# A four-layer attention kernel: the first pair's mask and matrix added by GpSimd to ScalarE's copy

## The chip, the cores and the metric

The kernel runs on one NeuronCore of a Trainium2 chip. The metric is the device time of one execution in microseconds (us), the median of several runs. The engines are TensorE (PE in the profile), VectorE (DVE), ScalarE (ACT), GpSimd (POOL) and SyncE (SP), which issues the DMAs.

## The reference

The network has four layers, each a cross attention followed by a feed-forward part, over 8 batches of 512 tokens with 256 features. Only the attentions of layers 0, 1 and 3 (the "masked layers") are touched:

```python
# layers 0 and 3: 16 heads of 16 features; layer 0 has a mask for each batch, layer 3 one for all
scores = einsum('bhqd,bhkd->bhqk', Q, K) / 4
scores = where(mask == 0, very_negative, scores)
attn = softmax(scores, axis=-1);  ctx = einsum('bhqk,bhkd->bhqd', attn, V)
out = ctx @ wo + bo
# layer 1: the same, but a matrix is added to the scores ahead of the mask
scores = scores + adj[None, None, :, :]
scores = where(mask == 0, -inf, scores)
```

## The kernel before, in words

`masked_attention` is called three times. It walks through 8 batches ("frames"); a frame has 16 steps, one for each pair of a group of four heads (four groups) and a block of 128 keys (four blocks). A step has two halves, so a frame has 32 positions p, with p = 2s + half. Half 0 works on the first pair of heads of the group, half 1 on the second.

A step s does this, all loops written out in the same order on each engine:

- Scores for the row maxima, seven steps ahead (`LEAD`): TensorE writes the scores of one head into one of two PSUM tiles `p1_ps` (L267), VectorE adds `bias` (mask, and matrix in layer 1), and takes the minimum of the negated sum (L420). TensorE may fill a tile only when VectorE is done with what was in it.
- Once for each group of heads VectorE splits the maxima into three bf16 parts (L363, L366, L369, L372, all at positions p % 8 == 2), TensorE turns them, ScalarE copies them to `m_row` (L459) and SyncE places them into `q_stack` (L599). The maxima are thereby subtracted within the next matmul.
- Scores for the probabilities: TensorE writes the transposed scores of a pair into `p2_ps[half]` (L281). In layers 0 and 3 it adds `biasT` with two more matmuls against the identity (L285), and ScalarE takes the exponential straight from PSUM into `probs` (L493). In layer 1 VectorE adds `biasT` on the way from PSUM to `probs` for both pairs (`BY_DVE`, L435), and ScalarE takes the exponential in place (L493).
- The sums over the keys (PV): at half 1 of step s TensorE multiplies `probs` of step s - 1 with the values into `oT_ps` (L295). It waits for both exponentials of step s - 1. The exponential of a pair waits until PV has read the buffer of two steps before.

Front work for the batch after next and end work for the batch before stand at fixed positions (`VALUES`, `FRONT`, `TAIL`, `MAXIMA`, `TURNED`), all through one PSUM tile `front_ps`, so that TensorE does the transposes and projections between its steps.

GpSimd has no part in the steps. Its queue runs by itself, in the order of `pool_frame` (L543): the four transposed masks of the next batch (`pool_mask`, L536, in layer 1 with L540), then for the batch after next the reciprocal root of the norm (L499, L501), the residual's bias (L507), the split of k into three bf16 parts (L517 to L523, for two halves), two masks, the split of q, two masks. SyncE's queue (`sp_frame`) loads masks into two buffers in turn, stores the parts (`sp_parts`, L572), reloads them as stacks (`sp_stack`, L583, six DMAs), and places the maxima. A mask is loaded only when GpSimd is done with the mask two before. VectorE takes the norm's statistics at position 18 and applies the norm at position 20 (L305, L309, L315); the apply waits for GpSimd's root.

## Time and profile before

| | us |
|---|---|
| median of 3 runs (lowest to highest) | 4907.16 (4906.79 to 4924.59) |
| the profiled execution's own time | 4903.92 |
| its span | 4902.2 |
| TensorE busy | 3380.4 (69%) |
| VectorE busy | 2923.2 (60%) |
| ScalarE busy | 1701.3 (35%) |
| GpSimd busy | 1121.8 (23%) |

The shares are means over very different stages. The attention of layer 0 runs from about 16 to 781 us of the span, that of layer 1 from 1307 to 2224, that of layer 3 from 3593 to 4355. Within each, the frames of the middle repeat themselves, so one frame of each layer says what bounds that layer; the last two frames have less front work.

### The profile page before, as it was taken

Reading aid. Unit: us, or ns where it says so; the run is one execution under the profiler, and the core shown is the slowest. Engines: PE = TensorE matmul, PEld = TensorE weight load, DVE = VectorE, ACT = ScalarE, POOL = GpSimd, SP = SyncE. Lnnn points to the kernel's source line nnn. Section 1 sums busy time; section 2 is a strip of 40 time slices with the busy share of each in tenths; the row PEclk is TensorE's granted clock in tenths of the full one; section 3 lists DMA queues with packets and bytes.
Section 4 is the critical chain, followed back from the end, with each engine's and each line's share of the span. In section 5 each row is a group of like instructions: output and inputs, shape, how many; then the busy total and the mean of one; then the engine's idle time right before and its main releaser. Section 6 shows DMA issues by size and latency. Waiting matters only on the chain. (4 is left out here: it accounts for less than half of the span.)

```text
span 4902.2 us, 66991 instructions
## 1 busy us (share of the span) xinstructions
PE 3380.4 (69%) x18245; PEld 1693.7 (35%) x18245; DVE 2923.2 (60%) x7895; ACT 1701.3 (35%) x2353; POOL 1121.8 (23%) x1003
## 2 busy tenths in 40 slices
PE   2999994222347777776966777777228999962598
PEld 1343432111112222223643445454113434332365
DVE  2665665888649878894224555555736666635711
ACT  0454553222114434442114555455103555530011
POOL 3443320111254434401101111110023121100032
PEclk7999997555669888897988888888558999975599
DMA  4635420000254434501027888887033425211033
GB/s 114 112 78 94 83 53 18 0 0 0 49 117 91 89 83 90 104 13 40 0 53 223 239 235 237 246 250 232 17 62 65 67 51 81 40 57 39 18 98 74
DMA packets 194490, 442.86 MB, mean 90 GB/s; under 512 B 25664, under 2 KB 77776, under 8 KB 187872
## 3 DMA queue, kind: packets, MB, share of 16 engines
q1 hardware_dynamic: 188000, 430.37, 37.0%
q0 software_dynamic: 6144, 8.39, 1.0%
q8 instruction: 154, 2.52, 0.2%
q14 instruction: 192, 1.57, 0.1%
HBM read 290.64 MB, written 146.85 MB: 89 GB/s over the span
## 5 line engine op out<-in xcount | busy, mean ns | idle before, releaser
L420 DVE CUSTOM_DVE_ANT_0 A_sums<-A_p_ps,A_bias 128x512 bf16<-128x512 f32 x1536 | 1005.8, 687 | 563.0 <-PE A_p_ps L267 540.7
L493 ACT ACTIVATE A_probs<-A_p_ps 128x1024 f32<-128x1024 f32 x512 | 523.4, 1024 | 548.6 <-PE A_p_ps L285 547.0
L267 PE MATMUL A_p_ps<-A_k_stack,A_q_stack 96*128 96x512 bf16 x1536 | 536.6, 399 | 208.1 <-DVE A_nmax L420 193.6
L281 PE MATMUL A_p_ps<-A_q_stack,A_k_stack 99*128 99x512 bf16 x1536 | 475.2, 391 | 5.6 <-DMA A_q_stack<-A_m_row 3.7
L295 PE MATMUL A_oT_ps<-A_probs,A_v_aug 128*17 128x512 f32 x3072 | 428.9, 632 | 6.5 <-ACT A_probs L493 4.3
L493 ACT ACTIVATE A_probs<-A_probs 128x1024 f32<-128x1024 f32 x256 | 270.7, 1057 | 428.9 <-DVE A_probs L435 428.4
L1072 DVE CUSTOM_DVE_ANT_0 A_scores<-A_qk_ps,A_rel_in 128x384 f32<-128x384 f32 (+3 forms) x512 | 232.5, 486 | 209.3 <-PE A_qk_ps L959 205.4
L267 PEld LDWEIGHTS A_p_ps<-A_k_stack,A_q_stack 96*128 96x128 bf16 x1536 | 139.5, 99 | 629.1 <-DVE A_nmax L420 528.4
L435 DVE TENSOR_TENSOR A_probs<-A_p_ps,A_biasT 128x1024 f32<-128x1024 f32 x256 | 311.6, 1219 | 2.0 <-PE A_p_ps L281 1.9
L285 PE MATMUL A_p_ps<-A_biasT,ident_bf 128*128 128x512 bf16 x1024 | 307.8, 381 | 0.0
L1117 ACT ACTIVATE A_rel_out<-A_rel_ps 128x1024 f32<-128x1024 f32 (+3 forms) x256 | 179.7, 702 | 339.4 <-DMA A_rel_dram<-A_rel_out 279.8
L1062 DVE COPY A_probsT<-A_t_ps 128x1024 f32<-128x1024 f32 (+3 forms) x256 | 210.6, 822 | 135.5 <-PE A_t_ps L982 129.7
L982 PE MATMUL A_t_ps<-ident,A_scores 128*128 128x128 f32 x1280 | 214.8, 304 | 86.4 <-DVE A_probsT L1062 81.0
L1124 ACT ACTIVATE A_scores<-A_scores,A_nmax 128x384 f32<-128x384 f32 (+3 forms) x512 | 257.1, 553 | 9.0 <-DVE A_nmax L1072 8.8
L222 PE MATMUL A_front_ps<-A_ctxT,A_wk 128*128 128x512 f32 x192 | 122.3, 771 | 178.6 <-DMA A_ctxT<-in_ctxT 163.5
L946 PE MATMUL A_rel_ps<-A_er_stack,A_q_stack 96*128 96x384 bf16 (+3 forms) x512 | 125.6, 330 | 153.0 <-ACT A_rel_out L1117 149.2
L536 POOL TENSOR_SCALAR A_biasT<-A_mask_in 128x512 bf16<-128x512 int32 (+2 forms) x68 | 130.7, 1922 | 361.1 <-DMA A_mask_in<-in_mask0T 183.3
L982 PEld LDWEIGHTS A_t_ps<-ident,A_scores 128*128 128x128 f32 x1280 | 151.9, 153 | 147.5 <-DVE A_probsT L1062 63.9
L281 PEld LDWEIGHTS A_p_ps<-A_q_stack,A_k_stack 99*128 99x128 bf16 x1536 | 148.8, 100 | 151.3 <-issue 19.7
L536 POOL TENSOR_SCALAR A_bias<-A_mask_in 128x512 bf16<-128x512 int32 (+2 forms) x68 | 131.5, 1933 | 149.2 <-DMA A_mask_in<-in_mask 98.0
L1444 POOL TENSOR_TENSOR B_act_out<-B_act_out,B_sc_bc 128x512 f32<-128x512 f32 x64 | 87.1, 1395 | 311.8 <-DVE B_sc_bc L1612 311.8
L1477 PE MATMUL B_h_ps<-B_xqT,B_w_q 128*128 (+1 forms) x128 | 51.6, 509 | 145.3 <-DVE B_hs L1574 144.3
(346 smaller groups left out, 5742.3 us busy)
## 6 DMA issues: line engine op xcount, KB each, us to landing
A_parts_dram<-A_parts SPq DMA_DIRECT2D x64, 768.0 KB, 4.6
A_k_stack<-A_parts_dram SPq DMA_DIRECT2D x192, 256.0 KB, 9.8
A_q_stack<-A_parts_dram SPq DMA_DIRECT2D x192, 256.0 KB, 8.9
A_rel_dram<-A_rel_out SPq DMA_DIRECT2D x64, 512.0 KB, 4.8
A_rel_in<-A_rel_dram SPq DMA_DIRECT2D x64, 512.0 KB, 5.2
A_rel_dram<-A_rel_out SPq DMA_DIRECT2D x64, 384.0 KB, 4.7
A_rel_in<-A_rel_dram SPq DMA_DIRECT2D x64, 384.0 KB
A_ctxT<-in_ctxT SPq DMA_DIRECT2D x32, 512.0 KB, 11.6
```

Of the source, the lines that this page charges most:

```text
L267: nc.tensor.matmul(p1_ps[i % 2][:, :], q_stack[0:KS, a_par, j * GH + i, t * P:(t + 1) * P], k_stack[0:KS, a_par, j * GH + i, :], start=Tru ...
L281: last = nc.tensor.matmul(p2_ps[half][:, i % 2, :], k_stack[:, par, j * GH + i, kb * P:(kb + 1) * P], q_stack[:, par, j * GH + i, :], star ...
L285: last = nc.tensor.matmul(p2_ps[half][:, i % 2, :], ident_bf[:, :], biasT[:, par % NB, kb, :], start=False, stop=True)
L295: nc.tensor.matmul(oT_ps[CW * i:CW * i + HD + 1, :], v_aug[:, v_par, kb, j * GH + i, :], probs[:, (s - 1) % 2 * 2 + i // 2, i % 2, :], sta ...
L420: nc.vector.tensor_tensor_reduce(out=sums[:, i % NX, :], in0=p1_ps[i % 2][:, :], in1=bias[:, (par + over) % NB, t, :], scale=-1.0, scalar= ...
L435: nc.vector.tensor_tensor(probs[:, s % 2 * 2 + half, :, :], p2_ps[half][:, :, :], turned, ALU.add).then_inc(biased, 1)
L493: nc.scalar.activation(dst, src, ACT.Exp).then_inc(exp_done, 1)
L536: last = nc.gpsimd.tensor_scalar(dst, mask_in[:, k % 2, :], 0.0, NEG, ALU.is_equal, ALU.mult)
L982: last = nc.tensor.transpose(t_ps[:, i, kb, :], scores[(p - TURN_LAG) % NP][:, i, kb * P:(kb + 1) * P], ident[:, :])
L1062: nc.vector.tensor_copy(probsT[u % NP][:, :, 0:nk, :], t_ps[:, :, 0:nk, :]).then_inc(copied, 1)
L1072: nc.vector.tensor_tensor_reduce(out=scores[p % NP][:, i, 0:n], in0=qk_ps[i][:, 0:n], in1=rel_in[s % NI][:, (2 * half + i) * n:(2 * half + ...
L1124: nc.scalar.activation(scores[u % NP][:, i, 0:n], scores[u % NP][:, i, 0:n], ACT.Exp, bias=nmax[:, u % NP, i:i + 1], scale=-1.0).then_inc( ...
```

## The change

One variable and what follows from it: in the masked layers the first pair (half 0) is no longer added to by TensorE (layers 0 and 3) or VectorE (layer 1). `BY_POOL` is `(0,)` in all three layers, and `BY_DVE` is `(1,)` in layer 1 and empty in the others. For the first pair ScalarE now copies `p2_ps[0]` into `probs` (a Copy of 128x1024), GpSimd adds `biasT` in place (`pool_add`), and ScalarE takes the exponential in place one step later, between its copy of the next step and the second pair's exponential. The second pair is as before in layers 0 and 3 (matmuls against the identity), and VectorE's in layer 1.

GpSimd's other work is placed step by step between the adds. The second half of q's split moves into the next frame (step 0), the norm's statistics move to position 12 and its apply to position 14, and SyncE stores q's parts behind the first group of maxima, just ahead of the reload of them.

```diff
-        BY_DVE = (0, 1) if adj is not None else ()
+        BY_POOL, BY_DVE = (0,), (1,) if adj is not None else ()
-        START = 16
+        START = 12
@@ pe_positions
-                    elif later(b * STEPS + s):
-                        pe.wait_ge(exp_done, b * HALVES + p - 1)
+                    elif half in BY_POOL:
+                        if later(b * STEPS + s):
+                            pe.wait_ge(p2_copied, b * STEPS + s)
+                    elif later(b * STEPS + s):
+                        pe.wait_ge(exp_done, b * HALVES + p - 2)
-                    if half not in BY_DVE:
+                    if half not in BY_DVE + BY_POOL:
@@ dve_positions
-                if has(b + 2, 0) and p == 18:
+                if has(b + 2, 0) and p == 12:
                     dve_norm_input(dve, b + 2)
-                if has(b + 2, 0) and p == 20:
+                if has(b + 2, 0) and p == 14:
                     dve_apply_norm(dve, b + 2)
@@ act_positions
+                if half in BY_POOL:
+                    if has(b, s):
+                        if later(b * STEPS + s - 1):
+                            act.wait_ge(pv_done, (b * STEPS + s - 1) * GH)
+                        act.wait_ge(p2_done, b * HALVES + p + 1).then_inc(apart_act, 1)
+                        nc.scalar.activation(probs[:, s % 2 * 2 + half, :, :], p2_ps[half][:, :, :], ACT.Copy).then_inc(p2_copied, 1)
+                    if has(b, s - 1):
+                        dst = probs[:, (s - 1) % 2 * 2 + half, :, :]
+                        act.wait_ge(pool_biased, b * STEPS + s).then_inc(apart_act, 1)
+                        nc.scalar.activation(dst, dst, ACT.Exp).then_inc(exp_done, 1)
+        def pool_add(pool, b, par, s):
+            if s == 0:
+                pool.wait_ge(bias_ready, (b + 1) * MK if every_mask else MK).then_inc(apart_pool, 1)
+            pool.wait_ge(p2_copied, b * STEPS + s + 1).then_inc(apart_pool, 1)
+            pair = probs[:, s % 2 * 2, :, :]
+            turned = biasT[:, par % NB, s % TPB:s % TPB + 1, :].to_broadcast([P, 2, S])
+            nc.gpsimd.tensor_tensor(pair, pair, turned, ALU.add).then_inc(pool_biased, 1)
@@ pool_frame
+            after, then = has(b, 0) and has(b + 1, 0), has(b + 2, 0)
+            for s in range(STEPS):
+                if has(b, s):
+                    pool_add(pool, b, par, s)
+                if after and s == 0:
+                    pool_split(pool, b + 1, 0, 1)
+                if has(b + 1, 0) and s == 7:
+                    pool_residual(pool, b + 1)
+                if after and every_mask and s in (2, 3, 5, 6):
+                    pool_mask(pool, b + 1, 1 - par, TPB + (2, 3, 5, 6).index(s))
+                if then and s == 6:
+                    pool_norm(pool, b + 2)
+                for at, which, i in ((10, 1, 0), (12, 1, 1), (15, 0, 0)):
+                    if then and s == at:
+                        pool_split(pool, b + 2, which, i)
+                if then and every_mask and s in (9, 11, 13, 14):
+                    pool_mask(pool, b + 2, par, (9, 11, 13, 14).index(s))
@@ sp_frame
             if after:
+                sp_parts(sp, b + 1, 0)
                 sp_stack(sp, b + 1, 1 - par, 0)
@@
-            if then:
-                sp_parts(sp, b + 2, 1)
             if masks_then:
                 for k in (2, 3):
                     sp_mask(sp, b + 2, k)
+            if then:
+                sp_parts(sp, b + 2, 1)
             if has(b + 1, 0):
                 sp_maxima(sp, b, par, 4)
-            if then:
-                sp_parts(sp, b + 2, 0)
```

GpSimd's queue in layer 0 before, from the transposed masks of the next batch (`A_biasT`) on to the first half of k's split:

```order
L536 TENSOR_SCALAR A_biasT<-A_mask_in 128x512 x4
L499 TENSOR_SCALAR A_rstd<-A_moments 128x4
L501 TENSOR_TENSOR A_rstd<-A_rstd,A_minus_half 128x4
L507 TENSOR_TENSOR x_sb<-x_sb,A_bo_bc 128x1024
L517 CAST A_parts<-A_qk 128x512
```

The same place now, steps 4 to 8 of a frame; the rows on `A_probs` are the new adds:

```order
L530 TENSOR_TENSOR A_probs<-A_probs,A_biasT 128x1024 x2
L558 TENSOR_SCALAR A_biasT<-A_mask_in 128x512
L530 TENSOR_TENSOR A_probs<-A_probs,A_biasT 128x1024
L558 TENSOR_SCALAR A_biasT<-A_mask_in 128x512
L513 TENSOR_SCALAR A_rstd<-A_moments 128x4
L515 TENSOR_TENSOR A_rstd<-A_rstd,A_minus_half 128x4
L530 TENSOR_TENSOR A_probs<-A_probs,A_biasT 128x1024
L521 TENSOR_TENSOR x_sb<-x_sb,A_bo_bc 128x1024
```

The masks, the root of the norm and the residual now stand between adds, which the steps wait for; the root stands behind two masks and the adds of steps 5 and 6.

SyncE's queue in layer 0 before, from the start of a frame on (`A_k_stack` and `A_q_stack` from `A_parts_dram` are the stacks of the next batch, `A_q_stack<-A_m_row` the maxima):

```order
L583 DMA A_k_stack<-A_parts_dram 16x8192 x6
L591 DMA A_mask_in<-in_mask0T 128x512 x2
L599 DMA A_q_stack<-A_m_row 3x512 x4
L583 DMA A_q_stack<-A_parts_dram 16x8192 x6
L591 DMA A_mask_in<-in_mask0T 128x512 x2
L565 DMA A_ctxT<-in_ctxT 128x2x512
```

And now:

```order
L615 DMA A_mask_in<-in_mask0T 128x512 x2
L623 DMA A_q_stack<-A_m_row 3x512 x4
L596 DMA A_parts_dram<-A_parts 128x3x1024
L607 DMA A_q_stack<-A_parts_dram 16x8192 x6
L615 DMA A_mask_in<-in_mask0T 128x512 x2
L589 DMA A_ctxT<-in_ctxT 128x2x512
```

The store of q's parts has come in between the first maxima and the reload of q's stack, and the last two transposed masks still follow that reload.

## Rows read from the trace of the kernel before

**Rows 1.** Windows, a frame each of layers 0, 1, 3, then five of layer 1.
```profile
core 0: us, PE busy (x) PEld busy (x) DVE busy (x) ACT busy (x) POOL busy (x), PEclk, DMA share, GB/s
553.40:636.30 82.90, 79.81 (x421) 32.67 (x418) 52.83 (x172) 42.24 (x49) 33.38 (x28) 1.00 0.47 92
1954.00:2058.00 104.00, 80.97 (x361) 28.71 (x354) 92.40 (x218) 43.33 (x49) 45.58 (x37) 0.89 0.46 97
4045.20:4127.80 82.60, 79.46 (x420) 33.55 (x416) 52.35 (x171) 42.26 (x49) 17.70 (x19) 1.00 0.39 65
...
1531.00:2058.00 527.00, 406.61 (x1757) 149.83 (x1758) 450.32 (x1043) 210.61 (x240) 214.79 (x175) 0.87 0.43 90
```
**Rows 2.** The page's costliest groups: the maxima, and layer 1's adds by VectorE.
```profile
L420 DVE CUSTOM_DVE_ANT_0 A_sums<-A_p_ps,A_bias 128x512 bf16<-128x512 f32 x1536 | 1005.8, 687 | 563.0 <-PE A_p_ps L267 540.7
...
L435 DVE TENSOR_TENSOR A_probs<-A_p_ps,A_biasT 128x1024 f32<-128x1024 f32 x256 | 311.6, 1219 | 2.0 <-PE A_p_ps L281 1.9
```
**Rows 3.** Timeline (start, duration, ...), TensorE, layer 0: a step with nothing between its halves.
```profile
636.22 0.61 PE L267 MATMUL A_p_ps<-A_k_stack,A_q_stack 96*128 96x512 bf16 x2
636.66 0.60 PE L281 MATMUL A_p_ps<-A_q_stack,A_k_stack 99*128 99x512 bf16 x2
...
638.20 0.39 PE L267 MATMUL A_p_ps<-A_k_stack,A_q_stack 96*128 96x512 bf16 x1 [0.22 <-DVE A_nmax L420]
...
639.39 1.05 PE L295 MATMUL A_oT_ps<-A_probs,A_v_aug 128*17 128x512 f32 x8
```
**Rows 4.** Timeline, layer 0: bias matmuls and their exponential; then the end.
```profile
594.24 0.59 PE L285 MATMUL A_p_ps<-A_biasT,ident_bf 128*128 128x512 bf16 x2
594.98 1.02 ACT L493 ACTIVATE A_probs<-A_p_ps 128x1024 f32<-128x1024 f32 x1 [1.36 <-PE A_p_ps L285]
...
772.10 1.02 ACT L493 ACTIVATE A_probs<-A_p_ps 128x1024 f32<-128x1024 f32 x1 [0.28 <-PE A_p_ps L285]
773.17 1.05 PE L295 MATMUL A_oT_ps<-A_probs,A_v_aug 128*17 128x512 f32 x8 [0.24 <-ACT A_probs L493]
774.37 0.60 ACT L482 ACTIVATE A_oT_sb<-A_oT_ps 128x512 f32<-128x512 f32 x1 [1.25 <-PE A_oT_ps L295]
```
**Rows 5.** Timeline, layer 0's frame from 553.4: SyncE, GpSimd, and step 8 on TensorE.
```profile
565.08 2.75 SPq L599 DMA_DIRECT2D A_q_stack<-A_m_row  x4
567.93 2.83 SPq L583 DMA_DIRECT2D A_q_stack<-A_parts_dram  x6
...
584.29 1.92 POOL L536 TENSOR_SCALAR A_biasT<-A_mask_in 128x512 bf16<-128x512 int32 x1 [9.62 <-DMA A_mask_in<-in_mask0T]
...
593.36 0.61 PE L267 MATMUL A_p_ps<-A_k_stack,A_q_stack 96*128 96x512 bf16 x2
...
605.26 1.04 POOL L501 TENSOR_TENSOR A_rstd<-A_rstd,A_minus_half 128x4 f32<-128x4 f32 x1
...
607.26 1.38 DVE L315 TENSOR_SCALAR A_xn<-x_sb,A_moments,A_rstd 128x256 f32<-128x256 f32 x4
```
**Rows 6.** The page's DMA issues, KB each, us from issue to landing.
```profile
A_parts_dram<-A_parts SPq DMA_DIRECT2D x64, 768.0 KB, 4.6
```
**Rows 7.** GpSimd's two-input operations by line: ns min/median/max.
```profile
L507 POOL TENSOR_TENSOR x_sb<-x_sb,A_bo_bc x24: 2342/2354/2380, 101.3 to 4183.1; 128x1024 f32<-128x1024 f32 x12, 128x1024 f32 x12
...
L540 POOL TENSOR_TENSOR A_biasT<-A_biasT,A_adj_in x32: 1262/1272/1297, 1387.8 to 2096.2; 128x512 f32<-128x512 f32 x32
```
**Rows 8.** Timeline of GpSimd and VectorE at one moment; then VectorE's splits by line.
```profile
285.79 1.16 POOL L519 TENSOR_TENSOR A_qk<-A_qk,A_parts 128x512 f32<-128x512 f32 x1
285.82 1.17 DVE L372 TENSOR_TENSOR A_m_parts<-A_m_rest,A_m_parts 128x16 bf16<-128x16 f32 x1
...
L363 DVE CAST A_m_parts<-A_nmax x96: 170/182/1162, 120.4 to 4326.2; 128x16 bf16<-128x16 f32 x96
L372 DVE TENSOR_TENSOR A_m_parts<-A_m_rest,A_m_parts x96: 170/186/1170, 123.4 to 4326.9; 128x16 bf16<-128x16 f32 x96
```
**Rows 9.** Timeline of TensorE in layer 0 behind a stall.
```profile
386.39 1.22 PE L267 MATMUL A_p_ps<-A_k_stack,A_q_stack 96*128 96x512 bf16 x2 [1.90 <-DVE A_nmax L420]
```

More of the change, by code:

```diff
@@ L144, in masked_attention @@
         biased = sem("biased")
+        p2_copied, pool_biased = sem("p2_copied"), sem("pool_biased")
         exp_done = sem("exp_done")
@@ L272, in pe_positions @@
                         pe.wait_ge(m_placed[j % 2], (b * (NG // 2) + j // 2 + 1) * GH * 16)
-                    if every_mask and p == 0 and len(BY_DVE) < 2:
+                    if every_mask and p == 1 and 1 not in BY_DVE:
                         pe.wait_ge(bias_ready, (b + 1) * MK)
@@ L482, in act_positions @@
                     nc.scalar.activation(oT_sb[:, :], oT_ps[:, :], ACT.Copy).then_inc(oT_read, 1)
-                if has(b, s):
+                if half in BY_POOL:
[8 more added lines that the diff above has]
+                        nc.scalar.activation(dst, dst, ACT.Exp).then_inc(exp_done, 1)
+                elif has(b, s):
                     dst = probs[:, s % 2 * 2 + half, :, :]
@@ new lines, in pool_split @@
+        def pool_split(pool, bn, which, i):
+            use = use_of(bn - 2, "qk"[which], i)
+            pool.wait_ge(front_read, use + 1).then_inc(apart_pool, 1)
+            if i == 0:
+                pool.wait_ge(parts_out, (bn * 2 + 1 - which) * 16).then_inc(apart_pool, 1)
+            step = (bn * 2 * DC + (1 - which) * DC + i) * 3
+            nc.gpsimd.tensor_copy(parts[:, 0, i, :], qk32[:, i, :]).then_inc(split_step, 1)
+            pool.wait_ge(split_step, step + 1)
+            nc.gpsimd.tensor_tensor(qk32[:, i, :], qk32[:, i, :], parts[:, 0, i, :], ALU.subtract).then_inc(split_step, 1)
+            pool.wait_ge(split_step, step + 2).then_inc(apart_pool, 1)
+            nc.gpsimd.tensor_copy(parts[:, 1, i, :], qk32[:, i, :]).then_inc(split_step, 1)
+            pool.wait_ge(split_step, step + 3)
+            nc.gpsimd.tensor_tensor(parts[:, 2, i, :], qk32[:, i, :], parts[:, 1, i, :], ALU.subtract).then_inc(parts_ready, 1)
@@ L543, in pool_frame @@
         def pool_frame(pool, b, par):
-            if has(b, 0) and has(b + 1, 0) and every_mask:
-                for k in range(TPB, MK):
-                    pool_mask(pool, b + 1, 1 - par, k)
-            if not has(b + 2, 0):
-                return
-            pool_norm(pool, b + 2)
-            pool_residual(pool, b + 2)
-            pool_split(pool, b + 2, 1)
-            if every_mask:
-                for k in (0, 1):
-                    pool_mask(pool, b + 2, par, k)
-            pool_split(pool, b + 2, 0)
-            if every_mask:
-                for k in (2, 3):
-                    pool_mask(pool, b + 2, par, k)
+            after, then = has(b, 0) and has(b + 1, 0), has(b + 2, 0)
[15 more added lines that the diff above has]
+                    pool_mask(pool, b + 2, par, (9, 11, 13, 14).index(s))
         def sp_ctx(sp, bn):
```

17 lines of the change are left out of this document (1 added, 16 removed).

## The prediction, made before the changed kernel ran

> **What bounds the kernel now.** I read the windows first, a frame of each masked layer. In layers 0 and 3 TensorE is busy 79.8 of 82.9 us and 79.5 of 82.6 us at a granted clock of 1.00 (2.4 GHz): these layers are bound by TensorE's in-order queue. In layer 1 VectorE is busy 92.4 of 104 us, TensorE 81.0 at a mean clock of 0.89, and five frames take 527 us, 105.4 each: VectorE is the bound there. GpSimd is busy 33.4, 45.6 and 17.7 us, ScalarE 42 to 43 us, so both look free [rows 1].
>
> Next the timeline of one step of layer 0 with no front work between its halves. It starts at 636.22; the first pair's two score matmuls start at 636.66, so two matmuls of 512 columns take 0.44 us of the queue, 0.22 each. The fourth matmul for the maxima, at 638.20, waited for VectorE, and PV starts at 639.39, 3.17 us into the step [rows 3]. VectorE takes 0.69 us and a short read for each maximum [rows 2]. So in such a step a matmul less in half 0 brings nothing; VectorE's pace sets the third and fourth. Where 1.9 us of front work stands between the halves, it brings its whole 0.44 us for the pair.
>
> Last I read SyncE, GpSimd and the chain at step 8 in the frame that starts at 553.4. The first maxima are issued from 565.08 to 567.83, the reload of q's stack at 567.93, and GpSimd starts the third transposed mask at 584.29, released by its DMA, 16.4 us after the reload's issue. Nobody waits for it now. Step 8 starts at 593.36, 40.0 us into the frame [rows 5].
>
> **The change part by part.**
>
> *Matmuls removed, layers 0 and 3.* 32 a frame, 7.0 us of queue at 0.22 us [rows 3]. Only the four steps with long front work between the halves (5, 8, 10, 14) give it back: -0.44 x 4 = -1.8 us a frame. The bounds are 0 and -7.0.
>
> *ScalarE's new chain.* In a plain step the first pair's last score matmul starts at +0.66. A pair's second bias matmul (594.24 + 0.22) was followed by ScalarE at 594.98, 0.52 us later, and a 128x1024 ScalarE operation takes 1.02 us; PV started 0.05 us behind its exponential's end (773.12 to 773.17) [rows 4]. So copy 1.18 to 2.20, exponential of the step before to 3.22, PV at 3.27 against 3.17 now: +0.1, and 0.05 more since an operation without a row of its own stands in the middle. Eleven steps, +1.6 us. With the -1.8 that is nothing. ScalarE has 42 us of work and gets 16 x 1.02 more, 59 of 83: not a bound.
>
> *The adds on GpSimd.* 16 a frame. The nearest row is the residual's add, also 128x1024 with a broadcast second input, 2.35 us; two of the matrix's adds are 2.54 us, the other end is 2.34 [rows 7]. I take 2.35: 37.6 us a frame. GpSimd then has 71 us in layer 0, 83 in layer 1, 55 in layer 3. An add starts at +2.2 of its step and is needed at about +2.2 of the next, 4.1 us or more later, so it has about 2 us to spare. That holds for splits and masks that are ready, not for a mask that isn't there.
>
> *Masks 6 and 7 and the norm, layer 0.* q's parts are now stored between 567.83 and the reload, and a store lands in 4.6 us [rows 6]. The reload is issued at 572.5 and the third mask lands 16.4 us behind it, at 588.9. GpSimd reaches it after the add of step 5, some 31 us into the frame (584.5), and stands there with the add of step 6 behind it. From 588.9: mask 1.92, add 2.35, mask 1.92, root 1.04 and a short add 0.25, gaps 0.5 between five operations: 596.9. VectorE waits there since its position 14 (about 591.5) for the root; then apply the norm 1.38, blocking 1.2 (below), one maximum 0.7: TensorE's first matmul of step 8 can start at 600.2 instead of 593.36, +6.9 us [rows 5, 7]. What comes behind has no slack in layer 0, so nothing is made up. Bounds: 0 (if masks land 8 us sooner than by this row) and +12 (if the store queues behind the k stack's loads too).
>
> *Cold TensorE.* It idles in two pieces before step 8. Behind an earlier stall two matmuls took 1.22 us for 0.61 and the clock was at 1.2 GHz [rows 9]; doubled pitches over some 3 to 6 us of work cost 0 to 3 us. I take 1.5.
>
> *VectorE against GpSimd.* At 285.79 GpSimd began a two-input operation of 1.16 us, and VectorE's split operation, begun at 285.82 and 0.186 us by its median, took 1.17 us: it ended with GpSimd's. The cast L363, with one input, has 182 ns by its median and up to 1162 [rows 8]. Now an add of 2.35 us stands in each step, and the four splits (p % 8 == 2) run their last operation at about +2.4, when the add has just begun. Such a block costs 0 to 2.35 us a split; a step's slack on VectorE (3.1 of 4.1 us) absorbs about half, so I take 1.0. In layers 0 and 1 two of four hide under the wait for the mask. The norm's apply, four operations that until now always ran while GpSimd waited for them, gets the adds beside it: 0 to 4.7, I take 1.2.
>
> The Trainium skill's page "SBUF — State Buffer", section "Who interferes with whom", says that a VectorE operation with two SBUF inputs, or a tensor_scalar or cast in a mode that uses both ports, is held for the whole of the GpSimd operation that came first. The rows agree for L372 and L363; none shows it for the apply. By the rule each apply would meet at least one whole add, 2.35 for my 1.2, and the time would be 21 us more (18 frames).
>
> *Layer 1.* VectorE loses 16 x 1.22 = 19.5 us a frame [rows 2]. Step 8 can start at: mask landed at 36.5, mask and matrix 3.2, add 2.35, mask and matrix 3.2, root 1.3, gaps 0.6, apply and block 2.6, maximum 0.7 = 50.4. Behind it GpSimd is the bound: 8 adds 18.8, 4 masks with matrix 12.8, 3 half splits 10.6 (two of 1.16 and two casts of about half), 30 gaps 3, and 4 us until its first copies come = 49. With 1.5 for the clock and 2 for split blocks: 102.9 against 105.4, -2.5 a frame. Bounds -12 (none of the waits) and +6.
>
> *The last two frames* have no front work. Layer 0: the mask is late for the seventh frame's step 6 (593.3 for 591.4, +1.9), 14 plain steps +2.1, blocks +1: +5. In the eighth, the last seven steps are a chain of copy, exponential, PV and its release (1.02 + 1.02 + 0.05 + 1.20 = 3.3 us, rows 4) where eight matmuls and PV were 1.76 + 1.05 = 2.8: +3.5, with nine plain steps and blocks +6. Layer 3: +9. Layer 1: -10, half of what VectorE could save.
>
> *What is moved at no cost:* the half split of q into step 0 and k's parts behind two masks; the k stack is needed at step 9 of the next frame, over 50 us later. START = 12 only lets the first norm be made earlier.
>
> **The sum.** Layer 0: 6.9 + 1.5 + 2.0 = 10.4 a frame, x6 = 62, + 11 = +73. Layer 3, without masks: four blocks 4.0 and the apply 1.2 = 5.2, x6 = 31, + 9 = +40. Layer 1: -15 - 10 = -25. Together +88 us on the profiled execution's 4903.9: 4992. The median of the runs is 3.3 us above that execution: **4995 us**.
>
> **The rivals.**
>
> *The waits don't come (faster).* The mechanism is GpSimd as a free adder: masks are there in time, VectorE is not held. For it: GpSimd is idle half of the frame now, and the mask's DMA alone is short. Against: the 16.4 us behind the reload and the order of SyncE's queue. Layers 0 and 3 then give 0 a frame and +7 each at the end; layer 1 drops 8.7 us a frame, -52, and -15 at the end: 4907 - 53 = 4854.
>
> *TensorE cools in layers 0 and 3 as it does in layer 1.* With 72.8 us of work in a frame and pieces of idle time in each step, a mean clock of 0.88 makes it 82.7, +9.9 a frame for 12 frames, on top of the sum: 4995 + 119 = 5114. For it: layer 1's 0.89 at 81 busy of 104. Against: its long waits, which layer 3 doesn't get.
>
> *No change.* The mask is late (+5.7 x 6 + 7 in layer 0), but blocks and cold stretches cost nothing, and layer 1 wins its 8.7 a frame: 41 + 7 - 52 = -4, 4903.
>
> **How the numbers follow.** The forecast has 0.56, with its own range of 4935 to 5060; faster 0.22, cold 0.10, no change 0.12. A measurement of this kernel can tell 0.5% (25 us) from no change. Faster by more: 0.22 and 0.02 of the last case, 0.24. Within: 0.10 of it and 0.03 of the forecast, 0.13. Slower: 0.63. The range reaches down to the faster case and up to near the cold one: 4852 to 5090.
>
> **What would show it.** GpSimd idle before the third transposed mask, released by its DMA, for about 4 us a frame in layers 0 and 1; VectorE idle before the norm's apply, released by the root, 5 us a frame in layer 0, and not in layer 3; step 8 starting 47 us into a frame of layer 0. The splits' maxima near 2.3 us, with means of 0.5 or more. Layer 3's frames at about 88 us, layer 1's at 103, GpSimd's adds at 2.35. The forecast is wrong if layer 0's frames stay at 83 us, or if layer 1 falls under 97.

## The result, and the profile after

The changed kernel takes **5122.41 us** (median of 4 runs, 5119.27 to 5124.22), the kernel before 4907.35 (4906.79 to 4924.59): a ratio of 1.044, 95% interval 1.042 to 1.046. The forecast was slower, 4995 us, with a range of 4852 to 5090. The direction was right, the size was not: +215 us for +88.

Where it went, from the first score matmul of a layer's first step to that of its last step (one profiled execution each; layer 1 repeats to some 7 us between kernels that are alike there, and 12 of the span's 219 us more fall outside these stretches):

| | layer 0 | layer 1 | layer 3 | sum |
|---|---|---|---|---|
| before | 638 | 775 | 633 | 2046 |
| changed | 723 | 853 | 677 | 2253 |
| difference | +85 | +78 | +44 | +207 |
| forecast | +73 | **-25** | +40 | +88 |

The windows of the changed kernel, one frame each of layers 0, 1 and 3 (columns as in [rows 1]):

```profile
core 0: us, PE busy (x) PEld busy (x) DVE busy (x) ACT busy (x) POOL busy (x), PEclk, DMA share, GB/s
618.60:713.30 94.70, 79.14 (x379) 30.84 (x384) 63.53 (x170) 56.54 (x64) 66.93 (x44) 0.93 0.41 78
1984.00:2096.90 112.90, 82.37 (x353) 32.08 (x352) 84.64 (x194) 55.79 (x64) 80.61 (x52) 0.86 0.40 85
4244.00:4332.80 88.80, 77.93 (x379) 31.36 (x384) 61.78 (x170) 56.52 (x64) 51.48 (x36) 0.96 0.37 61
```

In layer 1 no engine is full: VectorE 84.6 of 112.9 us, GpSimd 80.6, ScalarE 55.8. VectorE was to lose 19.5 us of work a frame and lost 7.8, on these frames (92.4 to 84.6, [rows 1]) and by its operations' durations over frames 2 to 6: an operation that is held, as below, counts as busy until it ends, so the norm's apply takes 3.9 us a frame more and the splits 6.3. TensorE's mean clock, 1.00 and 0.99 before in layers 0 and 3, fell to 0.93 and 0.96.

Two groups of VectorE's splits, which were at 0.18 to 0.19 us by their median in [rows 8], and TensorE's waits (columns: busy us, mean ns, then idle time ahead and what ended it):

```profile
L367 DVE CAST A_m_parts<-A_nmax 128x16 bf16<-128x16 f32 x96 | 84.9, 884 | 4.8 <-DVE A_nmax L424 3.9
L373 DVE CAST A_m_parts<-A_m_rest 128x16 bf16<-128x16 f32 x96 | 58.6, 611 | 0.1
...
L268 PE MATMUL A_p_ps<-A_k_stack,A_q_stack 96*128 96x512 bf16 x1536 | 561.8, 410 | 326.2 <-DVE A_nmax L424 309.9
...
L299 PE MATMUL A_oT_ps<-A_probs,A_v_aug 128*17 128x512 f32 x3072 | 440.1, 645 | 116.9 <-ACT A_probs L496 112.1
```

The timeline of layer 0's frame that starts at 618.6, masks, root and apply, on GpSimd, VectorE and TensorE:

```profile
654.25 1.92 POOL L558 TENSOR_SCALAR A_biasT<-A_mask_in 128x512 bf16<-128x512 int32 x1 [3.35 <-DMA A_mask_in<-in_mask0T]
...
656.25 2.13 POOL L530 TENSOR_TENSOR A_probs<-A_probs,A_biasT 128x1024 f32<-128x1024 f32 x1
...
658.47 1.92 POOL L558 TENSOR_SCALAR A_biasT<-A_mask_in 128x512 bf16<-128x512 int32 x1
...
660.79 1.04 POOL L515 TENSOR_TENSOR A_rstd<-A_rstd,A_minus_half 128x4 f32<-128x4 f32 x1
661.80 2.12 POOL L530 TENSOR_TENSOR A_probs<-A_probs,A_biasT 128x1024 f32<-128x1024 f32 x1
661.86 5.20 DVE L319 TENSOR_SCALAR A_xn<-x_sb,A_moments,A_rstd 128x256 f32<-128x256 f32 x4 [3.70 <-POOL A_rstd L515]
663.88 2.39 POOL L521 TENSOR_TENSOR x_sb<-x_sb,A_bo_bc 128x1024 f32<-128x1024 f32 x1
...
668.35 1.22 PE L268 MATMUL A_p_ps<-A_k_stack,A_q_stack 96*128 96x512 bf16 x2 [7.68 <-DVE A_nmax L424]
```

The third mask starts 35.65 us into the frame, where the forecast had 35.5, and GpSimd stood 3.35 us for it, where it had 4. What it missed is the apply: 5.20 us against 1.38 in [rows 5]. The first of its four operations is held by the add that began at 661.80, the second by the residual's add at 663.88; they took 2.21 and 2.42 us, the other two 0.40 each. In the kernel before the residual stood behind the apply of its own batch and could not meet it. Then the matmuls come at half speed: 1.22 us for two, the pattern of [rows 9].

Layer 1, from step 1 into step 2 of the frame that starts at 2096.9, all four engines:

```profile
2104.02 1.02 ACT L492 ACTIVATE A_probs<-A_p_ps 128x1024 f32<-128x1024 f32 x1 [1.54 <-PE A_p_ps L285]
...
2105.83 1.16 POOL L545 TENSOR_TENSOR A_parts<-A_qk,A_parts 128x512 bf16<-128x512 f32 x1
...
2106.94 2.36 POOL L530 TENSOR_TENSOR A_probs<-A_probs,A_biasT 128x1024 f32<-128x1024 f32 x1
2107.05 2.28 DVE L376 TENSOR_TENSOR A_m_parts<-A_m_rest,A_m_parts 128x16 bf16<-128x16 f32 x1
...
2110.47 1.21 DVE L439 TENSOR_TENSOR A_probs<-A_p_ps,A_biasT 128x1024 f32<-128x1024 f32 x1
...
2111.72 1.06 ACT L507 ACTIVATE A_probs<-A_probs 128x1024 f32<-128x1024 f32 x1 [5.73 <-DVE A_probs L439]
...
2112.68 0.57 ACT L463 ACTIVATE A_m_row<-A_front_ps 12x512 bf16<-12x512 f32 x1
...
2113.47 1.02 ACT L492 ACTIVATE A_probs<-A_p_ps 128x1024 f32<-128x1024 f32 x1 [0.22 <-ACT A_m_row L463]
...
2114.39 1.05 ACT L496 ACTIVATE A_probs<-A_probs 128x1024 f32<-128x1024 f32 x1
...
2115.49 1.91 PE L299 MATMUL A_oT_ps<-A_probs,A_v_aug 128*17 128x512 f32 x8 [1.62 <-ACT A_probs L496]
```

Read it from the top. The first pair's copy ends at 2105.04, but GpSimd is busy until 2106.99 with the half split of q that now stands in step 0. Then its add begins; VectorE's last split operation, 0.19 us of work, is held for 2.28 us. VectorE's next two maxima and its add for the second pair come that much later, and ScalarE, whose queue is in order, stands 5.73 us for them. The first pair's add had ended at 2109.30, but its exponential stands in the queue behind the second pair's exponential, the maxima's row and the next copy, and starts at 2114.39. PV (the sums over the keys) waits for it.

### The profile page after: what moved, and what is told of

Same layout as the page of the kernel before. It is cut to its first block and busy times, and to the rows that moved or that the text cites. A ratio compares the mean times of both kernels' runs of the same rounds, so it can differ in the third digit from the quotient of the medians.

```text
span 5121.4 us, 67623 instructions
## 1 busy us (share of the span) xinstructions
PE 3376.3 (66%) x17635; PEld 1675.8 (33%) x17733; DVE 3012.3 (59%) x7767; ACT 2042.0 (40%) x2737; POOL 1964.7 (38%) x1387
## 5 line engine op out<-in xcount | busy, mean ns | idle before, releaser
L530 POOL TENSOR_TENSOR A_probs<-A_probs,A_biasT 128x1024 f32<-128x1024 f32 x384 | 849.6, 2213 | 773.3 <-ACT A_probs L492 760.7
L268 PE MATMUL A_p_ps<-A_k_stack,A_q_stack 96*128 96x512 bf16 x1536 | 561.8, 410 | 326.2 <-DVE A_nmax L424 309.9
L492 ACT ACTIVATE A_probs<-A_p_ps 128x1024 f32<-128x1024 f32 x384 | 392.6, 1022 | 409.8 <-PE A_p_ps L285 388.0
L299 PE MATMUL A_oT_ps<-A_probs,A_v_aug 128*17 128x512 f32 x3072 | 440.1, 645 | 116.9 <-ACT A_probs L496 112.1
L285 PE MATMUL A_p_ps<-A_q_stack,A_k_stack 99*128 99x512 bf16 x1536 | 487.5, 402 | 0.5 <-DVE A_probs L439 0.5
L496 ACT ACTIVATE A_probs<-A_probs 128x1024 f32<-128x1024 f32 x384 | 403.3, 1050 | 3.9 <-POOL A_probs L530 2.7
L507 ACT ACTIVATE A_probs<-A_p_ps 128x1024 f32<-128x1024 f32 x256 | 262.0, 1023 | 122.5 <-PE A_p_ps L289 120.9
L507 ACT ACTIVATE A_probs<-A_probs 128x1024 f32<-128x1024 f32 x128 | 135.3, 1057 | 305.6 <-DVE A_probs L439 305.6
L223 PE MATMUL A_front_ps<-A_ctxT,A_wk 128*128 128x512 f32 x192 | 112.9, 718 | 170.2 <-DMA A_ctxT<-in_ctxT 162.2
L1004 PEld LDWEIGHTS A_t_ps<-ident,A_scores 128*128 128x128 f32 x1280 | 152.7, 154 | 149.5 <-DVE A_probsT L1084 62.7
L319 DVE TENSOR_SCALAR A_xn<-x_sb,A_moments,A_rstd 128x256 f32<-128x256 f32 (+1 forms) x96 | 98.1, 1082 | 151.4 <-POOL A_rstd L515 151.4
```

Of the source, the lines that this page charges most:

```text
L268: nc.tensor.matmul(p1_ps[i % 2][:, :], q_stack[0:KS, a_par, j * GH + i, t * P:(t + 1) * P], k_stack[0:KS, a_par, j * GH + i, :], start=Tru ...
L285: last = nc.tensor.matmul(p2_ps[half][:, i % 2, :], k_stack[:, par, j * GH + i, kb * P:(kb + 1) * P], q_stack[:, par, j * GH + i, :], star ...
L299: nc.tensor.matmul(oT_ps[CW * i:CW * i + HD + 1, :], v_aug[:, v_par, kb, j * GH + i, :], probs[:, (s - 1) % 2 * 2 + i // 2, i % 2, :], sta ...
L492: nc.scalar.activation(probs[:, s % 2 * 2 + half, :, :], p2_ps[half][:, :, :], ACT.Copy).then_inc(p2_copied, 1)
L496: nc.scalar.activation(dst, dst, ACT.Exp).then_inc(exp_done, 1)
L507: nc.scalar.activation(dst, src, ACT.Exp).then_inc(exp_done, 1)
```

## The experiments

The first kernels take the change apart; the later ones repair it. "Adds" are GpSimd's new operations. All ratios are to the kernel before, with 95% intervals. Layer figures are first to last step, as above; the expectations of e1 to e4 count a layer's whole attention instead (for layer 0 its end in the span), which is some 137, 135 and 125 us more in layers 0, 1 and 3. The layer figures come from the one profiled execution, the medians from all. In most kernels that execution lies within 7 us of the median, but in f1, g1 and h3 it was the slowest, 10, 15 and 16 us above it, in h1 the fastest, 11 below; their layer figures can be off by as much in sum.

| kernel | layer 0 | layer 1 | layer 3 | median us | ratio |
|---|---|---|---|---|---|
| e1 placing only | 676 | 812 | 641 | 4997 | 1.017 (1.015-1.020) |
| e2 one-input add | 700 | 793 | 651 | 5016 | 1.021 (1.018-1.024) |
| e3 small add | 683 | 762 | 632 | 4959 | 1.011 (1.009-1.014) |
| f1 delay, no hold | 694 | 794 | 643 | 5001 | 1.019 (1.017-1.022) |
| f2 hold, no delay | 720 | 816 | 654 | 5049 | 1.030 (1.027-1.032) |
| e4 norm between | 676 | 820 | 667 | 5033 | 1.026 (1.024-1.029) |
| f3 e4 without adds | 633 | 803 | 632 | 4931 | 1.005 (1.002-1.007) |
| g3 late norm, no adds | 636 | 778 | 632 | 4911 | 1.001 (1.000-1.002) |
| f4 e4, adds yield | 657 | 775 | 657 | 4961 | 1.012 (1.010-1.014) |
| g1 f4, late norm | 674 | 785 | 656 | 4970 | 1.013 (1.011-1.014) |
| g2 g1, adds in layer 1 alone | 635 | 792 | 632 | 4928 | 1.003 (1.002-1.005) |
| g4 f4, exponential first | 652 | 744 | 647 | 4924 | 1.005 (1.003-1.007) |
| h1 changed, exponential first | 714 | 816 | 663 | 5079 | 1.036 (1.034-1.038) |
| h2 g4, adds in layer 1 alone | 633 | 752 | 635 | **4883** | 0.995 (0.994-0.997) |
| h3 h2 without yielding | 633 | 768 | 634 | 4890 | 0.997 (0.995-0.998) |
| h4 h2, late norm | 635 | 761 | 635 | 4893 | 0.998 (0.997-1.000) |

**e1, the placing alone.** Besides this line, two waits of TensorE are set back to what they were.

```diff
-        BY_POOL, BY_DVE = (0,), (1,) if adj is not None else ()
+        BY_POOL, BY_DVE = (), (0, 1) if adj is not None else ()
```


> The new placing of masks, norm, splits and stores, without the adds on GpSimd: both pairs by TensorE in layers 0 and 3, by VectorE in layer 1, as in the kernel before. Stage lengths of the attentions of layers 0, 1, 3 were 775, 911, 756 us before and 864, 987, 806 changed. If the adds and what they hold up are the cause (hold, latency): layer 0 about 799 (the root still waits for masks that land late, +4 us in six frames), layers 1 and 3 within 5 us of 911 and 756, total 4925 to 4940. If the placing is the cause: layer 1 at 950 or more, layer 0 at 830 or more, total above 5000.

In those figures 813, 947 and 764 us: between the two cases, in layer 1 and in all nearer to the placing's. 83 of the 207 us come with no add at all. The timeline of layer 0, GpSimd and VectorE:

```profile
620.77 3.92 POOL L558 TENSOR_SCALAR A_biasT<-A_mask_in 128x512 bf16<-128x512 int32 x2 [14.19 <-DMA A_mask_in<-in_mask0T]
...
626.11 2.34 POOL L521 TENSOR_TENSOR x_sb<-x_sb,A_bo_bc 128x1024 f32<-128x1024 f32 x1
626.17 3.40 DVE L319 TENSOR_SCALAR A_xn<-x_sb,A_moments,A_rstd 128x256 f32<-128x256 f32 x4 [2.34 <-POOL A_rstd L515]
```

The late mask holds the root, and the residual's add holds the apply (3.40 for 1.38).

**e3, the small add.**

```diff
-            nc.gpsimd.tensor_tensor(pair, pair, turned, ALU.add).then_inc(pool_biased, 1)
+            nc.gpsimd.tensor_tensor(pair[:, :, 0:2], pair[:, :, 0:2], turned[:, :, 0:2], ALU.add)...
```


> GpSimd's add covers only 2 columns for each head (128x4; the first pair gets almost no mask and matrix), so neither a hold nor 2.1 us of latency nor GpSimd's load is left; ScalarE's copy, its order, and the late masks stay. 'Hold' and 'latency' both expect layer 0 at about 800 us (masks still late), layer 3 at 758, layer 1 at 880 or less, total 4880 to 4900. If ScalarE's copy and the order of its queue cost by themselves: layer 3 at 775 or more, layer 1 at 920 or more, total above 4940.

Layer 3 is at 632, with 633 before and 641 in e1, which has the same placing. So ScalarE's copy and the order of its queue cost nothing there when the add is short, and the removed matmuls bring something. On the mean of the first six frames, against e1, steps 5, 8, 10 and 14, with front work between their halves, are 0.3 to 0.4 us shorter each, and step 7 is 0.9 shorter, where the apply takes 1.38 for e1's 2.27 to 2.48; the eleven others together are 0.1 longer. Layer 0 keeps the placing's cost. Layer 1 is 50 us under e1: this is what VectorE's 19.5 us a frame are worth, the copy taken off. Against before the placing eats most of it: 897 us where I expected 880 or less.

**e2, an operation with one input.**

```diff
-            nc.gpsimd.tensor_tensor(pair, pair, turned, ALU.add).then_inc(pool_biased, 1)
+            nc.gpsimd.tensor_scalar(pair, pair, 1.0, 0.0, ALU.mult, ALU.add).then_inc(pool_biased, 1)
```


> GpSimd's add is replaced by an operation with one SBUF input over the same 128x1024 (times 1, plus 0; the first pair gets no mask and no matrix). Its duration isn't known, 1 to 3.8 us by the nearest rows. Theory 'hold' (two-input operations of VectorE and GpSimd exclude each other): the splits, layer 1's nan add and the norm's apply fall back to their medians (0.19 and 1.4 us for four), layer 0 at about 820 us, layer 3 at 772, layer 1 at 930, total 5000. Theory 'latency' (ScalarE's queue in order, copy, add, exponential, PV): layer 1 stays at 970 or more, total 5070 or more, unless the operation is much shorter than 2.1 us. Theory 'load' (GpSimd is simply full): total moves only as the operation's duration does.

The figures (837, 928 and 776; 5016) are near those of the hold theory, but not for its reason, so the run doesn't decide for it: this operation takes 1.04 us, half of the add's time, and it holds VectorE as well, until it ends. Layer 3 of e2:

```profile
4162.85 1.04 POOL L530 TENSOR_SCALAR A_probs<-A_probs 128x1024 f32<-128x1024 f32 x1 [0.48 <-ACT A_probs L492]
...
4162.93 0.99 DVE L370 TENSOR_TENSOR A_m_rest<-A_nmax,A_m_parts 128x16 f32<-128x16 f32 x1
```

**f1 and f2, delay and hold by themselves.** In f1 an int32 operation stands ahead of the small add; in f2 the small add stands ahead of a large two-input operation (1.97 us) in a spare tile. In both the first pair gets almost no mask and matrix.

The new operation of f1, ahead of e3's small add, then that of f2, behind it (both cut at the end, without the waits that order them):

```diff
+            nc.gpsimd.tensor_scalar(spare_out[:, :, :], spare_in[:, :, :].to_broadcast([P, 2, 240]), 0.0, NEG, ...
```
```diff
+            nc.gpsimd.tensor_tensor(spare_f[:, :, :], spare_f[:, :, :], turned[:, :, 0:500], ALU.add)...
```


> As the changed kernel, but in each step GpSimd first does an int32 operation of 128x480 into a spare tile (some 1.9 us; in all traces so far no VectorE operation that began beside the masks' int32 operation was held), then an add of 128x4 (0.2 us): the delay of the add of 2.1 us stays, the hold goes. The first pair gets almost no mask. From first to last step, layers 0, 1, 3 took 723, 853, 677 us in the changed kernel and 683, 762, 632 with the small add alone. If the hold makes the difference: within 10 us of 683, 775, 632, total 4960 to 4985. If the delay does (copy, add, exponential, PV in a row): 715, 845, 670, total above 5080.

> The mirror image: GpSimd does the add of 128x4, which releases ScalarE, and then a two-input operation of 128x1000 in a spare tile (about 2.1 us). The hold and GpSimd's load stay, the delay ahead of the exponential goes. If the hold makes the difference: layers 0, 1, 3 at 715, 840, 672, total 5080 to 5120. If the delay does: within 10 us of 683, 762, 632, total below 4985.

f1's int32 operation holds little: the split of 0.19 us runs through beside it. (Not all do, see the last section; the expectation's "no VectorE operation ... was held" is too strong.) Summed over the run, what the splits take beyond their own time is 37 us in f1, 18 in e3, 119 in f2 and 178 in the changed kernel.

```profile
140.66 1.83 POOL L532 TENSOR_SCALAR A_spare_out<-A_spare_in 128x480 bf16<-128x480 int32 x1
...
141.34 0.19 DVE L378 TENSOR_TENSOR A_m_parts<-A_m_rest,A_m_parts 128x16 bf16<-128x16 f32 x1
```

Both cost, over e3: the delay 11, 32 and 11 us, the hold 37, 54 and 22. Together 167, where the real add costs 40 + 91 + 45 = 176. By the medians it is 41 and 90, together 131 of 163. So of what the two stand-ins cost, hold is about two thirds and delay one third. That they add up to the whole is not shown: 9 to 32 us stay open, and neither stand-in is quite the add. Each forecast was pure and each was too pure.

**e4, the norm between two adds.** The root ahead of the third transposed mask, statistics at position 10, apply at 12.

```diff
+                if has(b + 2, 0) and p == 10:
+                    dve_norm_input(dve, b + 2)
                 if has(b + 2, 0) and p == 12:
-                    dve_norm_input(dve, b + 2)
-                if has(b + 2, 0) and p == 14:
                     dve_apply_norm(dve, b + 2)
...
+                if then and s == 5:
+                    pool_norm(pool, b + 2)
...
-                if then and s == 6:
-                    pool_norm(pool, b + 2)
```


> All work is done; the norm's statistics go to position 10, GpSimd's root ahead of the third transposed mask (step 5), the apply to position 12, where GpSimd is between two adds. Theory 'hold' with the late masks: the apply is no longer held by two adds and no longer waits behind masks, layer 0 8 us a frame less (about 815 to 825 for the stage), layer 3 2.5 us a frame less (790), layer 1 3 to 5 us a frame less (960), total 5030. If the late mask itself (GpSimd's queue stands, the adds behind it wait) is what counts: layer 0 gains 3 us a frame at most (845), total 5080 or more.

As the first case said (813, 955, 792 in its figures; 5033): against the changed kernel layer 0 is 47 us shorter, layer 1 34, layer 3 10. The apply is not free of holds there: in the six frames that have one it takes 1.38 to 4.00 us in layer 0, 1.71 to 4.53 in layer 1, and in layer 3 its 3.24 are no less than the 3.20 of the changed kernel. So layer 3's 10 us are not from a shorter apply; what they are I have not tested.

**f3 and g3, where the placing costs.** f3 is e4 without adds; g3 has the norm at positions 18 and 20 again, root behind step 9, without adds.

> The new placing without the adds, but with the norm's statistics at position 10, the root ahead of the third transposed mask, and the apply at position 12. With the root behind the masks this took 4997 us (676, 812, 641 us in layers 0, 1, 3 from first to last step; 638, 775, 633 before). If the placing's cost is VectorE waiting for a root that stands behind late masks: 640, 780, 633, total 4905 to 4925. If it is something else of the placing (the stores and reloads of q moved together, statistics at another place): 660 or more in layer 0, 800 or more in layer 1.

> The new placing without any adds on GpSimd, the norm back at positions 18 and 20. With the norm at positions 10 and 12 layer 1 took 803 us, with it behind the masks 812, in the kernel before 775. If the early norm is all of layer 1's loss by placing: 775 to 780, total 4900 to 4910. If the split of q moved into step 0, the masks' steps or the late store of q's parts share in it: 785 or more, total 4915 or more.

Layer 0's loss was the root behind late masks, with the apply that then met the residual's add: 633 in f3, 636 in g3. Layer 1 is at 803 in f3, where I expected 780 or a cause outside the norm, and at 778 in g3, within its scatter of the 775 of before. So without adds all the placing's loss is the norm's: the split of q in step 0, the masks' steps and the late store of q's parts cost nothing. Beside adds that isn't shown; above, the split of q delays one by 1.9 us. Why steps 5 to 7 are a dear place for it in layer 1, even with no wait for the root, I have not tested.

**f4, adds that yield.** In the four steps with a split, GpSimd waits until VectorE's split is through.

```diff
+            if s % 4 == 1 and has(b, s + 3):
+                pool.wait_ge(m_split, b * NG + (s + 3) // 4 + 1)
```


> All work is done; the kernel with the norm between adds (5033 us; 676, 820, 667 us) and one wait more: in the four steps with a split GpSimd starts its add only when VectorE's split of the maxima is through. If the holds of the splits are what is left in layers 0 and 3: layer 3 at 645 to 650, layer 0 at 655, layer 1 at 805, total 4980. If the later add costs as much as the hold did (its slack of some 2 us is used up): no gain, 5020 to 5050.

72 us less than e4 in all; layer 1 gains 45, more than the 15 I gave it, and layer 3 10, less. Only the add of the split's own step waits; the first cast (L367) is still held, by the add of the step before, with a mean of 0.87 us for 0.88 in the changed kernel. By line, all 96 of the split's last operation, ns min/median/max, changed kernel and then f4:

```profile
L376 DVE TENSOR_TENSOR A_m_parts<-A_m_rest,A_m_parts x96: 185/188/2290, 122.4 to 4538.4; 128x16 bf16<-128x16 f32 x96
```
```profile
L376 DVE TENSOR_TENSOR A_m_parts<-A_m_rest,A_m_parts x96: 185/186/1014, 123.0 to 4379.5; 128x16 bf16<-128x16 f32 x96
```

**g1 and g2.** g1 is f4 with the late norm; g2 is g1 with `BY_POOL` empty in layers 0 and 3.

> All work is done. The kernel whose adds yield to the splits (4961 us; 657, 775, 657 us from first to last step of layers 0, 1, 3), with the norm back where the kernel before had it (statistics at position 18, apply at 20; GpSimd's root behind the add of step 9). If the norm's place in steps 5 to 7 costs in layer 1 by itself: layer 1 at 755 to 765, layers 0 and 3 within 8 us of 657, total 4945. If only its order against the masks counted: 775, total 4955 to 4970; the apply will again meet adds, which by the hold theory costs 2 us a frame.

> The same kernel, but with GpSimd's adds in layer 1 alone; in layers 0 and 3 TensorE's matmuls against the identity do both pairs, as before the change. All work is done. By the theory that the removed matmuls bring nothing and the adds only cost there: layers 0 and 3 at 633 to 642 and 632 to 638, layer 1 as in the kernel with adds everywhere (755 to 775), total 4885 to 4905, so level with the kernel before or 0.4% faster. If the adds of layers 0 and 3 weren't their cost: total above 4930.

g1 gained nothing: 9 us more by the medians. In layer 0 it is at 674 for 657, but this is the execution that was 15 us above its median, so how much the late apply costs beside adds is not settled. g2 gives layers 0 and 3 back, 635 and 632, so there the adds cost more than the matmuls they replace; layer 1 at 792 was 7 over the same code in g1. With 4928 it stayed slower than before, where I expected it level.

**g4 and h1, the exponential first.**

```diff
                 if half in BY_POOL:
+                    if has(b, s - 1):
+                        dst = probs[:, (s - 1) % 2 * 2 + half, :, :]
+                        act.wait_ge(pool_biased, b * STEPS + s).then_inc(apart_act, 1)
+                        nc.scalar.activation(dst, dst, ACT.Exp).then_inc(exp_done, 1)
                     if has(b, s):
... (the copy of step s, unchanged; the four lines above are taken out behind it)
```


> All work is done. The kernel whose adds yield (4961 us), with ScalarE's order changed: the exponential of the first pair of step s - 1 ahead of the copy of step s. The row copy 1.0, add 2.1, exponential 1.05, copy becomes a closed ring of 4.3 us, while PV is released 1 us sooner. If PV's wait for that exponential (8.9 us a frame in layer 1) is latency that the order makes: layer 1 10 to 20 us shorter, total 4940 to 4950. If the ring binds: steps of the last two frames at 4.3 us instead of 3.76, layers 0 and 3 at 665 or more, total above 4975.

> All work is done. The changed kernel with one edit: ScalarE takes the exponential of the first pair of step s - 1 ahead of the copy of step s. In the kernel whose adds yield the same edit gained 5, 30 and 10 us in layers 0, 1 and 3. If the order makes the add's delay cost, independent of the holds: about the same gains here, so 717, 820, 665 us (now 723, 853, 677), total 5070 to 5085. If a hold and a late exponential are needed together: more, total below 5060. If it only works once the holds are gone: within 10 us of 5122.

g4 gains 37 us over f4, 30 of them in layer 1, where I expected 10 to 20; even layers 0 and 3 gain, though the ring does bind in the last frame: 15 steps in 65.1 us, 4.34 each, for 62.7. h1 gains 43 us on the changed kernel by the medians; its profiled execution is 55 under that of the changed kernel, 37 of them in layer 1. So the order's cost is there with the holds too. The page's group for PV, f4 and then g4:

```profile
L299 PE MATMUL A_oT_ps<-A_probs,A_v_aug 128*17 128x512 f32 x3072 | 438.1, 642 | 121.5 <-ACT A_probs L496 116.0
```
```profile
L299 PE MATMUL A_oT_ps<-A_probs,A_v_aug 128*17 128x512 f32 x3072 | 437.3, 642 | 69.2 <-ACT A_probs L491 67.5
```

**h2, h3 and h4, adds in layer 1 alone.** h2 is g4 with `BY_POOL = (0,)` in layer 1 and `()` elsewhere; h3 drops the yielding, h4 puts the norm late.

> All work is done. GpSimd's adds in layer 1 alone, yielding to the splits, exponential ahead of the copy, norm at positions 10 and 12; layers 0 and 3 without adds. By the parts measured so far: 633, 745, 631 us in layers 0, 1, 3 (before: 638, 775, 633), 37 us less than the kernel before, total 4865 to 4885. If the gain of the exponential's order hung on layers 0 and 3, or layer 1 behaves as in the other kernel with adds there alone (792 for 785): total 4890 to 4920.

> As the kernel with adds in layer 1 alone and the exponential first, without the wait that lets the splits go ahead of the adds. If holds cost by themselves: layer 1 at 775 to 790 (the yielding brought 45 us with the copy first), total 4905 to 4920. If the holds only hurt through ScalarE's old order: layer 1 at 745 to 755, total as with the wait.

> As the kernel with adds in layer 1 alone, yielding, exponential first, but with the norm's statistics at position 18 and its apply at 20. With the copy first the late norm cost 10 us in layer 1 (785 for 775), without any adds it brought 24 (778 for 803). If the apply beside adds decides: layer 1 at 755, total 4880 to 4895. If the early norm's place decides: 730, total 4855 to 4870.

h2 is faster than both kernels, if by little: 4883.16 us, 0.5% under the one before (0.3 to 0.6), within the 4865 to 4885 expected; layer 1 is at 752, where I expected 745. Its windows for layers 0, 1 and 3:

```profile
552.91:635.27 82.36, 79.54 (x417) 32.56 (x416) 53.46 (x170) 42.09 (x48) 33.22 (x27) 1.00 0.49 91
1931.61:2023.99 92.38, 74.22 (x353) 27.14 (x352) 78.94 (x194) 55.84 (x64) 80.09 (x52) 0.94 0.49 104
4113.26:4195.44 82.18, 79.44 (x418) 32.53 (x416) 53.76 (x170) 42.09 (x48) 19.79 (x20) 1.00 0.40 66
```

GpSimd has the same 80 us of work in layer 1 as in the changed kernel, in a frame of 92.4 us instead of 112.9. That is one of h2's shortest; the mean of frames 2 to 6 is 100.3 us, against 115.4 in the changed kernel and 105.7 before. h3's layer 1 is 16 us longer, but its profiled execution was 16 above its median, and the medians are 7 apart with intervals that overlap. So the yielding's worth is not settled there; it is well under the 45 of f4, so with the better order the steps absorb most of the holds. h4 costs 10 us by the medians, with intervals that don't overlap: beside adds the early norm is the better one, as g1 already leaned.

## Why the prediction was wrong, step by step

**The step that failed is layer 1**, "102.9 against 105.4, -2.5 a frame" and "Layer 1: -10" for the last two frames; measured 115.4 a frame (mean of frames 2 to 6) and +14. The forecast split the frame at step 8: first at 50.4 us, then 52.5 more. The second half was right: 53.4. The first was 62.0. I had made it one chain from the landing of a mask at 36.5, and taken what comes before as free. In none of frames 2 to 6 did GpSimd wait for that mask, and the start is late all the same:

```profile
2137.66 1.92 POOL L558 TENSOR_SCALAR A_biasT<-A_mask_in 128x512 f32<-128x512 int32 x1
...
2148.20 2.36 POOL L530 TENSOR_TENSOR A_probs<-A_probs,A_biasT 128x1024 f32<-128x1024 f32 x1
2148.26 5.43 DVE L319 TENSOR_SCALAR A_xn<-x_sb,A_moments,A_rstd 128x256 f32<-128x256 f32 x4 [1.36 <-POOL A_rstd L515]
...
2155.19 1.22 PE L268 MATMUL A_p_ps<-A_k_stack,A_q_stack 96*128 96x512 bf16 x2 [5.32 <-DVE A_nmax L424]
```

The mask starts 40.8 us into this frame: the steps ahead were late. They were late by splits held for up to 2.3 us, and by ScalarE's order, which carries VectorE's lateness over to the first pair. The repairs give their sizes in layer 1: norm between adds 34 us, yielding 45, exponential first 30. That is 109, and the forecast missed 103 there. That the two are so near is partly luck: the sizes hang on the order in which the repairs were made, each has the scatter of one execution, the new place of the norm is among them and costs 28 us in layer 1 without any adds (f3), and some holds remain.

**Adds, "2.35 us each".** 2.14 us in layers 0 and 3, where `biasT` is bf16, 2.36 in layer 1. Right within a tenth.

**"An add ... has about 2 us to spare."** Wrong as a rule for every step. f1 shows the delay almost alone at 54 us by its trace, 41 by the medians. That the slack is only that of a step in which nobody is late is my reading, not measured.

**Split blocks, "I take 1.0".** Right in sum in layer 3, but wrongly spread: against e3, on the mean of the first six frames, steps 1 and 13 are 2.1 and 1.9 us longer, the other two steps with a split (5 and 9) not at all, so 4.0 in all. In layer 0 the sum had 2.0, two of the four being hidden; steps 1 and 13 are 1.8 and 1.3 longer. I had four candidates and counted the last one; the first cast is held too, by the add of the step before (mean 0.88 us, above).

**The apply, "0 to 4.7, I take 1.2".** In its six frames of each layer it took 5.05 to 5.43 us in layers 0 and 1, where 1.38 was its own: 3.7 to 4.1, near the upper bound. In layer 3 it took 3.2, 1.8 more: three of its four operations ran before an add began. The Trainium skill's page "SBUF — State Buffer", section "Who interferes with whom", by which a tensor_scalar in a mode that uses both ports is held for the whole of the GpSimd operation that came first, was the better guide. The trace agrees: the operations above that began 0.06 and 0.11 us behind an add of 2.12 and of 2.39 us ended 0.15 us behind it. The int32 operations in the last section held for a part of their time only; there the measurement decides. In layers 0 and 1 the apply met the residual's add as well.

**"Masks 6/7 and the norm": +6.9 and a cold 1.5.** The waits were about as said. On the mean of frames 2 to 6 step 8 came at 52.8 us, 11.7 behind the kernel before (41.1; the 40.0 I used is one frame), for the 6.9 said. Of that miss 2.6 us are the apply's and some 2 step 1's. The clock cost more than 1.5: against layer 3 of e3, at 0.99 with the same matmuls, TensorE was busy 592 for 567 us in layer 0 and 588 in layer 3, 3 us a frame more, at a mean clock of 0.94 and 0.96: some of the matmuls ran at 1.2 instead of 2.4 GHz. Not all of it reached the frame's length: behind step 8 the frame is 1.6 us longer than before, for 3.5 in the sum.

**The tail, "1.02 + 1.02 + 0.05 + 1.20 = 3.3 us".** Its steps took 3.76. ScalarE's copy waits for the first pair's own matmuls, and these stand behind PV in TensorE's queue, which is in order too; I had left them out of the ring. Even so the last two frames came to +9 and +7 in layers 0 and 3, for +11 and +9. TensorE in layer 3, PV's starts 3.76 apart:

```profile
4552.28 1.05 PE L299 MATMUL A_oT_ps<-A_probs,A_v_aug 128*17 128x512 f32 x8 [1.30 <-ACT A_probs L496]
4553.27 1.04 PE L285 MATMUL A_p_ps<-A_q_stack,A_k_stack 99*128 99x512 bf16 x4
...
4556.04 1.05 PE L299 MATMUL A_oT_ps<-A_probs,A_v_aug 128*17 128x512 f32 x8 [1.30 <-ACT A_probs L496]
```

**Matmuls removed and ScalarE's chain, "nothing"** in layers 0 and 3. Nearly: of the -1.8 us a frame e3 shows -1.4 against e1 in layer 3 (above), and the +1.6 for the chain is at most 0.1 in any plain step. So the two together save about a microsecond a frame.

**What was moved at no cost:** right without adds for q's split, the parts' store and the masks (g3). The norm's new place cost 83 us (e1 against g3): 40 in layer 0, where the sum has its wait for the root, and 34 and 9 in layers 1 and 3, where it has next to nothing for the place.

**The rivals.** The free adder never came: even without hold and delay, e3 is at 4959. TensorE cooled, but to 0.94 and 0.96, not 0.88. The 5114 us of that rival lie 8 from the 5122 measured by chance: its 119 us were to come in layers 0 and 3, and those were 16 over the sum. As for the forecast's signs, GpSimd's wait for the third mask came in layer 0 (3.2 to 5.3 us a frame, for 4) and in layer 1 only in the first and the seventh frame. "The forecast is wrong if ... layer 1 falls under 97" looked to the wrong side; nothing in the list named a layer 1 above 103.

## What to carry to other kernels

Work moved to GpSimd is not only GpSimd's time: list every VectorE operation that can meet it and charge the whole of the other's duration, or make the two take turns, as the yielding adds do. Where an engine with an in-order queue gets one more stage, write down the queue of one step with its waits and let one input be 2 us late: what stands behind it is the price, and the order within the queue decides it. And let no root or small result that another engine waits for stand behind a DMA-bound operation.
